# Cross-attention contexts turned by VectorE from blocks, in place of transposes on TensorE

## The reference

```
x = x + xattn(layernorm(x), ctx, Wq, Wk, Wv, Wo, bo)
x = x + attn(layernorm(x), Wq, Wk, Wv, Wo, rel_bias_emb)
x = x + ffn(layernorm(x), clip_x, clip_down, w_gate, w_up, w_down)

# xattn, the part that the change touches: 16 heads of 64
q, k, v = h @ Wq, ctx @ Wk, ctx @ Wv
probs = softmax(q k^T / 8)          # 32 queries x 257 keys per batch and head
out = (probs v) @ Wo + bo
```

## Time and profile before

| | |
|---|---|
| time, median of 3 runs (lowest, highest) | 1582.34 us (1581.54, 1584.12) |
| span of the profiled execution, first to last instruction | 1580.3 us |
| TensorE busy | 1543.1 us, 98% |
| VectorE busy | 1066.2 us, 67% |
| ScalarE busy | 737.1 us, 47% |
| GpSimd busy | 371.2 us, 23% |
| mean granted TensorE clock | 0.995 |
| DMA, share of the 16 engines' span | 36.9% |

### The profile page before, as it was taken

The page is one execution under the profiler, slowest core; times in us unless marked ns, Lnnn a source line. Parts: engine busy times, 40 slices in busy tenths (PEclk is TensorE's granted clock), DMA queues, the critical chain, the costliest instruction groups (busy, mean ns, idle before and its releaser), DMA issues.

```text
span 1580.3 us, 36115 instructions
## 1 busy us (share of the span) xinstructions
PE 1543.1 (98%) x13802; PEld 1287.0 (81%) x13802; DVE 1066.2 (67%) x2306; ACT 737.1 (47%) x1596; POOL 371.2 (23%) x225
## 2 busy tenths in 40 slices
PE   7999899999999999999999999999999999998989
PEld 6888788988999899888988898878878878786544
DVE  8766677677666766776667766657555664556788
ACT  5444656455545554555545554433123222224755
POOL 1000235343444344343434344400000000000000
PEclk9999999999999999999999999999999999999999
DMA  6898864341334223431434133250311311223022
GB/s 241 318 369 345 328 238 139 125 154 57 125 138 138 90 92 138 138 133 58 141 127 153 54 128 124 81 200 22 107 63 35 115 49 42 99 84 134 1 107 107
DMA packets 78958, 210.74 MB, mean 133 GB/s; under 512 B 5712, under 2 KB 31760, under 8 KB 76048
## 3 DMA queue, kind: packets, MB, share of 16 engines
q1 hardware_dynamic: 78864, 209.39, 36.9%
HBM read 140.42 MB, written 68.94 MB: 132 GB/s over the span
## 4 chain that ended last, share of the span: by engine, by line
PE 75%; issue 12%; DVE 8%; ACT 4%; DMA 0%; DVEq 0%; SPq 0%; ACTq 0%; POOLq 0%; POOL 0%
PE psum_o L694 13%; PE psum_s L671 7%; PE psum_q L671 7%; PE psum_o L1488 6%; PE psum_q L1528 6%; PE psum_q L1488 6%; PE psum_t L1560 6%; PE psum_o L559 5%; PE psum_o L709 5%; DVE qk L1092 3%; PE psum_t L682 3%; PE psum_t L640 2%; PE psum_s L1515 1%; PE psum_t L591 1%; PE psum_q L591 1%
## 5 line engine op out<-in xcount | busy, mean ns | idle before, releaser
L694 PE MATMUL psum_o<-pT,c_nat 128*128 128x512 f32 x1152 | 307.3, 403 | 3.4 <-issue 2.4
L694 PEld LDWEIGHTS psum_o<-pT,c_nat 128*128 128x128 f32 x1152 | 202.7, 189 | 38.7 <-DVE pT L957 3.6
L1304 POOL TENSOR_TENSOR c_nat<-c_raw,constants 128x768 fp32r<-128x768 f32 x64 | 93.8, 1466 | 560.1 <-PE psum_o L694 445.3
L1158 DVE TENSOR_SCALAR oT<-psum_o,c_last 128x512 f32<-128x512 f32 x192 | 143.7, 748 | 65.5 <-PE psum_o L694 65.5
L671 PE MATMUL psum_s<-cT,qk 128*128 128x256 f32 (+1 forms) x1152 | 167.7, 288 | 2.3 <-DVE cT L957 0.3
L671 PEld LDWEIGHTS psum_s<-cT,qk 128*128 128x128 f32 x1152 | 151.0, 189 | 11.3 <-DVE cT L957 5.2
L671 PE MATMUL psum_q<-cT,qk 128*128 128x256 f32 (+1 forms) x1152 | 152.8, 284 | 1.0 <-DVE qk L1092 1.0
L884 ACT ACTIVATE probs<-psum_s,nmax 128x257 f32<-128x257 f32 x128 | 61.1, 477 | 197.7 <-DVE nmax L1173 197.7
L671 PEld LDWEIGHTS psum_q<-cT,qk 128*128 128x128 f32 x1152 | 143.3, 190 | 4.0 <-issue 2.6
L957 DVE TENSOR_TENSOR pT<-psum_t,pT 128x512 fp32r<-128x512 f32 x128 | 87.8, 687 | 70.9 <-ACT pT L775 70.9
L1289 POOL TENSOR_TENSOR c_raw<-c_raw,last_row 128x768 f32<-128x768 f32 x64 | 120.3, 1881 | 29.5 <-DMA last_row<-in_ctx_dram 19.1
(11 more groups left out here) (295 smaller groups left out, 3118.2 us busy)
## 6 DMA issues: line engine op xcount, KB each, us to landing
qk_by_tile<-staged SPq DMA_DIRECT2D x32, 1536.0 KB, 10.1
raw<-qk_by_tile SPq DMA_DIRECT2D x16, 3072.0 KB, 12.3
c_raw<-in_ctx_dram SPq DMA_DIRECT2D x64, 384.0 KB, 3.3
last_row<-in_ctx_dram SPq DMA_DIRECT2D x64, 192.0 KB, 4.0
out_dram<-x_out SPq DMA_DIRECT2D x32, 256.0 KB, 2.0
x_res<-in_x_dram SPq DMA_DIRECT2D x16, 256.0 KB, 2.7
x_in<-out_dram SPq DMA_DIRECT2D x4, 1024.0 KB, 8.5
x_all<-out_dram SPq DMA_DIRECT2D x1, 4096.0 KB, 13.3
```

The costliest lines, as they stand in the source:

```text
L694: i = pe.matmul(ps[:], c_nat[(b - 1) % 2][:, part, k, m * P:(m + 1) * P], pT[:, moving, k, :], start=(k, part, moving) == (0, 0, 0), stop= ...
L1158: nc.vector.tensor_scalar(oT[:, m, :, (b - 1) % 4, :], ps[:].rearrange("p (s q) -> p s q", q=SQ), c_last[:, (b - 1) % 2, m:m + 1], None, A ...
```

## The change

The context that the scores need is no longer made by TensorE. SP loads it a second time into c_blk by four DMAs (load_blocks): partition 32 f + n holds, for the keys 32 k + n, the features 96 f to 96 f + 95, so a piece of a row is 96 numbers, 384 bytes, and a context has 1024 pieces. One instruction of VectorE (dve_turn, STREAM_TRANSPOSE) turns all 32 × 32 blocks into cT_raw, at the head of the step before the first row maximum; its input takes every third feature, so that its steps are 12 bytes. ScalarE writes the last key's column (act_last_column, 6 numbers a partition, twice the same) and rounds 128 × 774 into the high part (act_context_high), GpSimd subtracts the low part (pool_context_low; in the first tile VectorE). Since the turned context is the raw one, all score groups have 258 columns, the last key's with them. c_raw less its last key stays for the attended sums.

Room is made in the on-chip memory: last_row has one buffer instead of two, so that load_ctx waits for pool_less_last; x_out goes, the result is written in place into x_res and stored from there, and the next x_res is loaded at the head of the next tile, when that store is done. The rows of Wk are read in another order to fit the new order of features, and the last keys are transposed in both orders once.

```diff
 def pe_scores(pe, t, b, rg, section):
-            if section == "first" and rg == 0 and b < 2:
-                pe.wait_ge(s_zero, b + 1)
+            if rg == 0:
+                pe.wait_ge(s_ctlo, 4 * t + (b + 1))
...
-            keys = SKP if section == "first" or (b, rg) == (0, 3) else 2 * P
             for c in range(KC):
-                if rg == 0:
-                    wait_chunk(pe, t, b, section, c)
                 for part, moving in PARTS:
-                    m = pe.matmul(ps[:, 0:keys], qk[:, part, rg, c, b, :], cT[b % 2][:, moving, c, 0:keys],
+                    m = pe.matmul(ps[:, 0:SKP], qk[:, part, rg, c, b, :], cT[b % 2][moving][:, c, :],
 def pe_cross_tile(pe, t, section):
...
                     pe_pv(pe, t, b, 0, section)
-                if before and (more or b < 3):
-                    pe_ctxT(pe, t, b, section, (0, 1))
-                if before:
                     pe_pv(pe, t, b, 1, section)
                 if b == 3 and begun:
                     pe_wo(pe, t, section)
-                if before and (more or b < 3):
-                    pe_ctxT(pe, t, b, section, (2,))
+        def act_last_column(act, batch, ahead):
+            nc.scalar.activation(cT_raw[ahead % 2][:, :, 2 * P:SKP], last_key(1, batch, ahead).to_broadcast([P, KC, 2]),
+                                 ACT.Copy).then_inc(s_lastcol, 1)
+        def act_context_high(act, batch, ahead):
+            act.wait_ge(s_lastcol, batch + (ahead + 1))
+            act.wait_ge(s_turn, batch + (ahead + 1))
+            nc.scalar.activation(cT[ahead % 2][0][:], cT_raw[ahead % 2][:], ACT.Copy).then_inc(s_cthi, 1)
 def act_cross_tile(act, t, section):
...
                 exp(b, 0)
+                if after:
+                    act_last_column(act, 4 * t, b + 1)
                 for k in range(2):
                     act_probsT(act, t, b, k, section)
+                if after:
+                    act_context_high(act, 4 * t, b + 1)
                 if b == 3 and more:
                     act_qk_high(act, t + 1, 0)
                 exp(b, 1)
+        def dve_turn(dve, batch, ahead):
+            dve.wait_ge(s_blk, 64 * batch + 64 * (ahead + 1))
+            nc.vector.transpose(cT_raw[ahead % 2][:, :, 0:2 * P].rearrange("p c (k n) -> p c k n", n=KEYS),
+                                c_blk[:].rearrange("p k (i c) -> p c k i", c=KC)).then_inc(s_turn, 1)
 def dve_x_out(dve, t, section):
...
-            dve.wait_ge(s_out, 16 * t)
-            nc.vector.tensor_tensor(x_out[:], ps[:], x_res[:], ALU.add).then_inc(free, 1)
+            nc.vector.tensor_tensor(x_res[:], ps[:], x_res[:], ALU.add).then_inc(free, 1)
+        def pool_context_low(pool, batch, ahead):
+            pool.wait_ge(s_cthi, batch + (ahead + 1))
+            nc.gpsimd.tensor_tensor(cT[ahead % 2][1][:], cT_raw[ahead % 2][:], cT[ahead % 2][0][:].bitcast(F32),
+                                    ALU.subtract).then_inc(s_ctlo, 1)
+        def load_blocks(sp, batch, ahead):
+            if not isinstance(batch, int) or batch + ahead:
+                sp.wait_ge(s_turn, batch + ahead)
+            keys = ctx_of(batch, ahead)
+            for f in range(4):
+                quarter = keys[:, 0:2 * P, f * QUARTER:(f + 1) * QUARTER]
+                sp.dma_start(c_blk[KEYS * f:KEYS * (f + 1), :, :],
+                             quarter.rearrange("a (k n) d -> n (a k) d", n=KEYS)).then_inc(s_blk, 16)
 def load_ctx(sp, batch, ahead):
+            if not isinstance(batch, int) or batch + ahead:
+                sp.wait_ge(s_sub, batch + ahead)
...
 def sp_cross_tile(sp, t, section):
             for b in range(4):
+                if b == 0 and section != "second":
+                    load_x_res(sp, t)
                 if more or b < 2:
+                    load_blocks(sp, 4 * t, b + 2)
                     sp.wait_ge(s_nat, 4 * t + (b + 1))
                     load_ctx(sp, 4 * t, b + 2)
```

More of the change, by code:

```diff
@@ L80, in cross_units @@
             u.append((("WO",), "q1"))
-        if not (section == "last" and b == 3):
-            u += [(("CT", b, c), ("t0", "t1")[c % 2]) for c in range(3)]
     return u
@@ L256, in build_kernel @@
         cT1_at = sb.at
-        cT1 = sb("cT1", [P, 2, KC, SKP], F32R)
+        cT1 = [sb(f"cT1_{part}", [P, KC, SKP], F32R) for part in ("low", "high")]
         c_nat1 = sb("c_nat1", [P, 2, 2, DC], F32R)
@@ L288, in build_kernel @@
         cT0_at = sb.at
-        cT0 = sb("cT0", [P, 2, KC, SKP], F32R)
+        cT0 = [sb(f"cT0_{part}", [P, KC, SKP], F32R) for part in ("low", "high")]
         c_nat0 = sb("c_nat0", [P, 2, 2, DC], F32R)
@@ L609, in pe_start_weights @@
                 m = pe.transpose(ps[:, c * NB:(c + 1) * NB], rem_rows[:, c * P:(c + 1) * P], ident[0:NB, 0:NB])
+            for c in range(KC):
+                m = pe.transpose(ps[:, (KC + c) * NB:(KC + c + 1) * NB],
+                                 rem_rows[:].rearrange("b (q c) -> b c q", c=KC)[:, c, :], ident[0:NB, 0:NB])
             m.then_inc(done, 1)
@@ L726, in pe_cross_tile @@
         def pe_cross_tile(pe, t, section):
-            begun, more = section != "first", section != "last"
+            begun = section != "first"
             for b in range(4):
@@ L827, in act_last_scalars, with last_key @@
                 taken(act, U1(("PV", b - 1, 2), t, section))
[L828 to L831, removed]
+            nc.scalar.activation(c_last[:, b % 2, :].rearrange("p (c a) -> p c a", a=1), last_key(0, 4 * t, b),
+                                 ACT.Copy).then_inc(s_last, 1)
+        def last_key(order, batch, ahead):
+            later = rem_all[:, order, :, ahead:]
+            return later[:, :, batch:batch + 1] if isinstance(batch, int) else later[:, :, bass.ds(batch, 1)]
+        def act_last_column(act, batch, ahead):
[5 more added lines that the diff above has]
+            nc.scalar.activation(cT[ahead % 2][0][:], cT_raw[ahead % 2][:], ACT.Copy).then_inc(s_cthi, 1)
         def act_project_all(act):
@@ L860, in act_project_all @@
                 act_qk_high(act, 0, rg)
-        def act_start_context(act, c):
-            act_high(act, project(("CT", "start", c)), cT[0][:, 0, c, 0:2 * P], cols(2 * P))
         def wo_quarter(ap, k):
@@ L890, in scale @@
                                      scale=rden[:, rg:rg + 1]).then_inc(s_scaled, 1)
-            def ctxT(b, c):
-                act_high(act, U1(("CT", b, c), t, section), cT[(b + 1) % 2][:, 0, c, 0:2 * P], cols(2 * P))
             if not begun:
+                full(act, project(("QK", GROUPS - 1, 7, KC - 1, 1)))
+                act_last_column(act, 4 * t, 1)
                 exp(0, 0)
                 exp(0, 1)
-                ctxT(0, 0)
-                ctxT(0, 1)
+                act_context_high(act, 4 * t, 1)
                 scale(0, 0)
-                ctxT(0, 2)
                 exp(0, 2)
@@ L927, in act_cross_tile @@
                     act_qk_high(act, t + 1, 1)
-                if after:
-                    ctxT(b, 0)
-                    ctxT(b, 1)
                 act_last_scalars(act, t, b, section)
-                if b == 3 and not begun:
-                    ctxT(b, 2)
                 if b == 3 and not more:
@@ L938, in act_cross_tile @@
                     act_qk_high(act, t + 1, 3)
-                if after and (b < 3 or begun):
-                    ctxT(b, 2)
         def act_cross_tail(act):
@@ L1126, in dve_project_all @@
                 else:
-                    for c in range(2):
-                        dve_start_context(dve, c)
-                    nc.vector.memset(cT[0][:, :, :, 2 * P:SKP].bitcast(F32), 0.0).then_inc(s_zero, 1)
+                    dve_turn(dve, 0, 0)
                 for j in range(4, 8):
@@ L1208, in dve_cross_tile @@
                 qk_next = b == 3 and more
+                if after:
+                    dve_turn(dve, 4 * t, b + 1)
                 row_max(b, 0)
@@ L1344, in pool_cross_tile @@
                 pool_split(pool, t, b, section)
+                if section != "last" or b < 3:
+                    pool_context_low(pool, 4 * t, b + 1)
                 if section != "last" or b < 3:
@@ L1408, in sp_project_all @@
                     if (s, j) == (GROUPS - 1, 4):
-                        full(sp, project(("CT", "start", 2)))
+                        load_blocks(sp, 0, 1)
                         sp.wait_ge(s_nat, 1)
@@ L1416, in sp_project_all @@
                 sp.wait_ge(s_staged[i], 32 * GROUPS)
-            full(sp, U1(("CT", 0, 2), 0, "first"))
+            load_blocks(sp, 0, 2)
             sp.wait_ge(s_nat, 2)
@@ L1420, in sp_project_all @@
             load_qk(sp, 0, 1)
+            load_blocks(sp, 0, 3)
             sp.wait_ge(s_nat, 3)
```

122 lines of the change are left out of this document (50 added, 72 removed).

## The result

The changed kernel takes 1629.6 us (median of 4 runs, 1629.0 to 1631.7), the kernel before 1582.2 beside it. The ratio is 1.030 (95% interval 1.028 to 1.031): slower by 47 us, where 16 less were forecast.

What follows compares the result with a forecast made beforehand. TensorE, busy 199.6 of 200 us, bounds the cross stage. Gains of 14 × 1.01 = 14, 1 (last tile) and 1 (first) take the span from 1580.3 to about 1564; with 2.0 to the median, 1566, range 1543 to 1600.

Steps and rivals of the forecast that it cites:

- the schedule: Hand layout of five engine queues for some tiles; for the kernel before it gave 51.31 us a tile, 51.37 measured.
- the first tile with the project stage also 1: First tile and project stage together: an estimated gain of 1 us.
- I cost both at nothing: SP's four block issues ahead of the natural context's load, and that load's wait for GpSimd: no cost.
- the loop's 50.30 a tile: Forecast tile, steps 11.24 + 14.50 + 9.14 + 15.42 us, 1.01 less than 51.31.
- The turn: taken as 0.98: VectorE's 128x768 turn ahead of the first row maximum: 0.98 us, bounds 0.71 and 1.78.
- Rival C: Dear turn on VectorE: at 1.8 us 1602, or 1594 if held until GpSimd's split ends; chance 0.18.
- The transposes: taken as 0.90 a batch: Six context transposes leaving TensorE: 0.56 + 0.34 = 0.90 us a batch, at most 58 us over 64 contexts.
- rival D: Pieces cost 5 us a batch; blocks behind the 3 MB of qk make b=2's turn 2 us late: 1603; chance 0.06.
- rival B: TensorE keeps the whole 0.90 us a batch: 1525; chance 0.10.
- The exclusion of the two engines: In b=3 VectorE's two-input subtractions wait for GpSimd; the first qk one moves from 6.33 to 8.67 us after the head.
- Rival A: GpSimd and VectorE don't exclude each other here: tile 49.32, 1552 us in all; chance 0.12.
- the cover of an ordinary step: Slack of 0.58 us before PV0's first load; in b=2 the turn leaves PV0 at 5.30 against TensorE's 5.27.

Runs made afterwards that it cites:

- The load order: Changed kernel with the blocks of contexts 2, 3 and 4 issued ahead of the first tile's waits for stores, qk and weights: 1614.9 us.
- the late turn: Changed kernel with VectorE's turn moved behind the first row maximum of a step: 1580.9 us.
- the larger pieces: Changed kernel with the blocks loaded in 128 pieces of 3072 bytes a context in place of 1024 of 384: 1625.6 us.
- the fastest kernel: Changed kernel with earlier first-tile blocks, turn behind row maximum, its input in runs of 32, b=3's less_last at next tile's head, next qk issued in b=1: 1553.1 us.
- moving GpSimd's work: Less_last of b=3 moved to the next tile's head, in the kernel with earlier first-tile blocks and turn behind row maximum (1564.6 us): 1560.6 us.

## Why the prediction was wrong

Between the forecast of 1566 and 1629.6 lie 63.6 us: 25 in the first tile with the project stage, 6 in the second, 31 in the loop (13 × (52.67 − 50.30), of which 1 is only that the schedule lay 0.06 a tile below the kernel before) and 2 elsewhere. The second tile's 6 were not followed further than to its clock of 0.94.

**The failed step: "the first tile with the project stage also 1".** It was not laid out. The tile took 23.9 us more, so this term alone misses by 25. What SP had to wait for at the start could be read in the diff: the blocks were put behind the wait for the stores, the qk load and the weights, and the single buffer lets no blocks be fetched ahead. The prediction said of these issues "I cost both at nothing" with an eye on the loop alone. The load order gave 15 of it back. This is the largest single term, but without it the time would still have been about 1604: the loop's 50.30 a tile failed too, by the three things that follow.

**The turn: taken as 0.98, measured 1.25.** The value was right for neighbouring numbers (0.97), so the rest is the steps of 12 bytes. By the prediction's own figures for a dearer turn (50.96 at 1.2, 51.56 at 1.4) 1.25 gives 51.11 a tile in place of 50.30, 0.81 × 13 = 11 us in the loop; taking it out gave 13 in all. That is still below 51.31: by the schedule the turn alone would have made the kernel no slower. Rival C had this mechanism, with a larger size. The Trainium skill ("SBUF — State Buffer", in "Door 1: The DMA port swizzle") says that fp32 numbers can be read in steps of up to four for free. This turn, with steps of three, does not agree (1.25 against 0.97); the same page's other rule, two hits in each 16-byte line for full bandwidth, agrees in direction and gives no size.

**The transposes: taken as 0.90 a batch, measured 0.66.** The 0.90 counts 1.28 for each attended group, as read behind transposes. Without the transposes the three groups stand behind one another. Their 18 loads in a step b=2 of the late turn, and the head of the next step:

```profile
637.96 4.05 PEld L670 LDWEIGHTS psum_o<-pT,c_nat 128*128 128x128 f32 x18
...
642.05 0.19 PEld L647 LDWEIGHTS psum_s<-cT_high,qk 128*128 128x128 f32 x1
```

They take 4.09 us, about 1.3 for the first group and 1.4 for each of the others, in place of 3 × 1.28 = 3.84. With the transposes it had been 4.75 (624.61 to 629.36). So 0.66 a batch could be won there. Why a group takes longer behind another one is not shown. With 0.25 for this and 0.27 for the turn the schedule's b=2 becomes 9.14 + 0.52 = 9.66 and its b=0 11.24 + 0.52 = 11.76; the undisturbed steps took 9.62 and 11.75. By the same account b=1 came out 0.1 longer and b=3 some 0.3 shorter, which stays open.

**What the schedule did not have.** With a turn of 1.25 it says 51.11; a tile of the loop with neither wait nor fallen clock takes 51.6, the mean tile 52.67. The 0.5 between the first two, 7 us of the loop's 31, lie in the dearer attended groups and, for 0.14, in the wider score groups. Between 51.6 and 52.67 lie the clock, 5 × 1.5 = 8 us over the 13 tiles, and b=2's waits for blocks, some 5: both follow from b=0 and from the place behind the 3 MB of qk (rival D's place, though not its price, as the larger pieces show). A fall of the clock stood nowhere in the prediction. In the loop before, no load of TensorE stood for more than 0.34 us, and the clock was 1.00.

**What held.** Most of the 0.90 a batch was there to be won: with the turn hidden b=2 takes 9.39 in place of 10.00, and the fastest kernel's tile of 48.85 is 2.5 below the 51.37 of before. The whole 0.90 of rival B never came. The exclusion of the two engines was right in place and size: the subtraction ended where the schedule had it, and moving GpSimd's work gave b=0 the 0.8. Rival A is refuted by that. ScalarE's rounding (0.86, forecast 0.92), GpSimd's subtraction (1.85) and the wider groups (0.14 a tile, allowed 0.2) were as forecast. The statement that the cover of an ordinary step "is used up to the last hundredths" was the warning that the place at the head was wrong: VectorE's 1.12 us of idle time, one instruction later, stood in the same trace.

## What to carry to other kernels

Lay out the first iteration by itself: a load that is free in the steady state can stand behind everything else at the start. When work moves to another engine, ask not only how long it is but which idle time of that engine's list it could fall into; here one line's move was worth 49 us. A price read from an engine's list holds for the neighbours that it had: take something out, and lay out again what then stands side by side. After each such gain look again at the queue that feeds it, since a shorter step brings loads into each other's way.

## What the runs showed of the hardware

A turn of 32 × 32 blocks, 128x768 in float32, takes 0.97 us from neighbouring numbers and 1.25 from every third. It runs beside GpSimd's subtractions without a delay (1.19 to 1.26 in all 64 cases, 60 of which overlap with GpSimd's work), while a VectorE subtraction with two inputs from the on-chip memory does not (2.51 in place of 1.75). Pieces of 384 bytes cost little more than pieces of 3072 (2.6 and 2.4 us for 96 KB). An idle time of TensorE of 2.3 us was followed by the lower clock in some tiles and not in others; of 1.1 us in none. Six attended products take 1.28 us behind transposes and 1.4 behind six others of their kind.
